# Layer 2 of a two-layer kernel on one core: the shifted copies of the values wait for the sorted rows, and four expert tiles' weights are fetched ahead of them

## The reference

```python
v = silu(causal_dwconv(hidden_states @ W_v, conv_w_v))        # q and k alike
vc = v.reshape(b, l, H * DV)
fir_s = causal_dwconv(vc, fir_short_w)      # 3 taps
fir_l = causal_dwconv(vc, fir_long_w)       # 31 taps
delta_out = delta_rule_chunkwise(q, k, v, beta)   # chunks of 32 rows, a scan over 8 chunks
gate_in = concatenate([hidden_states, fir_s, fir_l, delta_out], -1)
...
# experts: top 2 of 8 for every row
weights, indices = top_k(softmax(x @ router), 2)
out = sum over the two of  norm_weight * (silu(x @ gating[e]) * (x @ up[e])) @ down[e]
```

## Time and profile before

| | us |
|---|---|
| median of 3 runs | 667.78 (666.35 to 669.98) |
| profiled execution, first to last instruction (span) | 664.4 |
| PE busy | 517.5 (78%) |
| DVE busy | 423.6 (64%) |
| ACT busy | 223.4 (34%) |
| POOL busy | 208.5 (31%) |

### The profile page before, as it was taken

The page is one execution under the profiler, slowest core; times in us unless marked ns, Lnnn a source line. Parts: engine busy times, 40 slices in busy tenths (PEclk is TensorE's granted clock), DMA queues, the critical chain, the costliest instruction groups (busy, mean ns, idle before and its releaser), DMA issues.

```text
span 664.4 us, 17841 instructions
## 1 busy us (share of the span) xinstructions
PE 517.5 (78%) x7511; PEld 357.0 (54%) x7511; DVE 423.6 (64%) x861; ACT 223.4 (34%) x402; POOL 208.5 (31%) x170
## 2 busy tenths in 40 slices
PE   5636788888898889874869951789889889998962
PEld 4424566666666666652434420375458666656751
DVE  6897678686869696967456004947871123646796
ACT  2212444353344444350402102332222224424670
POOL 3472220303040404045512771382221111321470
PEclk9666799999999999998759995979995899898996
DMA  7375113131422332101100533154662343211216
GB/s 229 101 227 169 58 56 112 57 111 56 132 92 62 108 100 98 48 10 36 33 1 24 146 97 96 28 152 121 180 183 67 101 127 97 84 59 32 80 47 185
DMA packets 77838, 63.15 MB, mean 95 GB/s; under 512 B 9520, under 2 KB 70864, under 8 KB 77760
## 3 DMA queue, kind: packets, MB, share of 16 engines
q1 hardware_dynamic: 67840, 51.25, 26.6%
q0 software_dynamic: 3296, 7.02, 3.4%
q10 hardware_dynamic: 6624, 3.76, 2.1%
HBM read 44.42 MB, written 12.90 MB: 86 GB/s over the span
## 4 chain that ended last, share of the span: by engine, by line
PE 47%; DVE 18%; issue 10%; another core or an unknown queue 6%; ACT 5%; POOL 2%; DMA 1%; SPq 1%; DVEq 0%; ACTq 0%; POOLq 0%
PE ps L1045 5%; PE ps L874 5%; PE ps L914 4%; DVE small L1227 3%; PE ps L907 3%; DVE small L1190 3%; DVE BIG L1195 3%; PE ps L943 2%; PE ps L882 2%; PE ps L1054 2%; PE ps L769 2%; PE ps L822 2%; PE ps L732 2%; DVE BIG L1068 2%
## 5 line engine op out<-in xcount | busy, mean ns | idle before, releaser
L1863 POOL TENSOR_TENSOR BIG<-BIG,small 128x2048 f32<-128x2048 f32 x14 | 50.8, 3633 | 189.9 <-DVE small L1203 189.9
L1924 POOL DMA_INDIRECT home<-BIG x39 | 38.7, 992 | 140.0 <-ACT BIG L1806 125.0
L1068 DVE STREAM_TRANSPOSE BIG<-BIG 128x512 f32<-128x512 f32 (+3 forms) x30 | 25.6, 875 | 45.7 <-remote 44.9
L1045 PE MATMUL ps<-BIG 128*128 128x128 f32 x312 | 48.4, 305 | 3.3 <-ACT BIG L1638 3.3
L943 PE MATMUL ps<-BIG 128*32 128x512 f32 x256 | 32.5, 626 | 21.7 <-issue 21.7
L1045 PEld LDWEIGHTS ps<-BIG 128*128 128x128 f32 x312 | 43.9, 216 | 6.7 <-ACT BIG L1638 3.8
L874 PEld LDWEIGHTS ps<-BIG 128*128 128x128 f32 x368 | 44.7, 192 | 3.3
L874 PE MATMUL ps<-BIG 128*128 128x128 f32 x368 | 44.8, 275 | 0.0
L1694 ACT ACTIVATE BIG<-ps 128x1024 f32<-128x1024 f32 x32 | 31.0, 1022 | 36.6 <-PE ps L822 36.6
L1190 DVE TENSOR_REDUCE small<-ps 128x64 f32<-128x1024 f32 x32 | 39.0, 1219 | 6.2 <-PE ps L769 6.2
L1227 DVE TENSOR_REDUCE small<-ps 128x8 f32<-128x1024 f32 x32 | 37.7, 1219 | 7.9 <-PE ps L800 6.3
(11 more groups left out here) (264 smaller groups left out, 1114.9 us busy)
## 6 DMA issues: line engine op xcount, KB each, us to landing
BIG<-in_w SPq DMA_DIRECT2D x23, 512.0 KB
BIG<-in_w SPq DMA_DIRECT2D x23, 256.0 KB
BIG<-in_wg SPq DMA_DIRECT2D x39, 128.0 KB
BIG<-in_wu SPq DMA_DIRECT2D x39, 128.0 KB
BIG<-in_wd SPq DMA_DIRECT2D x39, 128.0 KB
BIG<-BIG SPq DMA_DIRECT2D x64, 71.4 KB
rows<-BIG SPq DMA_DIRECT2D x3, 936.0 KB
BIG<-rows ACTq DMA_DIRECT2D x39, 72.0 KB, 2.6
```

The source lines that it names most:

```text
L1045: t = e.matmul(bank(s)[:, i:i + 128], WT[(NTL[0] + j) % NWT][:, i:i + 128], XsT[(NTL[0] + j) % 2], start=True, stop=True)
L1068: return e.transpose(dst, src)
L1863: e.tensor_tensor(v, v, bc_last(zz[i], 16), ALU.mult).then_inc(p_ready, 1)
L1924: e.indirect_dma_start(YSd[1], bass.IndirectOffsetOnAxis(ap=XR[j % NXR][:, 128:129].bitcast(I32), axis=0), YS[J % 3], None).then_inc(d_hom ...
```

## The change

Two edits. The step `stack` gets one more wait, for all of the second 16 scatters. And SP's list is put in another order: `x1.2` and `x1.3` come ahead of all copies, the 16 DMAs of pair 0 come together ahead of the 16 of pair 1 (before, they alternated), and `x1.4`, `x1.5` and `x1.6` now stand each ahead of the copy that they stood behind. The list from `stack.2.3 x1.7` on is the same.

```diff
 TWO_SP = """
-x1.0 x1.1 stack.0.0 stack.1.0 x1.2 stack.0.1 stack.1.1 x1.3 stack.0.2 stack.1.2 stack.0.3 stack.1.3 stack.2.0 x1.4 stack.2.1 x1.5 stack.2.2
+x1.0 x1.1 x1.2 x1.3 stack.0.0 stack.0.1 stack.0.2 stack.0.3 stack.1.0 stack.1.1 stack.1.2 stack.1.3 x1.4 stack.2.0 x1.5 stack.2.1 x1.6 stack.2.2
...
                 if s[0] == "stack":
                     _, c, i = s
                     w.wait_ge(pad_ready, 1)
+                    w.wait_ge(d_scat[1], SCAT_ALL[1])
                     w.wait_ge(psum.empty(("pj", 2, c)))
                     if c >= 2:
                         w.wait_ge(psum.full(("fs", c - 2)))
```

More of the change, by code:

```diff
@@ L178 @@
 TWO_SP = """
-x1.0 x1.1 stack.0.0 stack.1.0 x1.2 stack.0.1 stack.1.1 x1.3 stack.0.2 stack.1.2 stack.0.3 stack.1.3 stack.2.0 x1.4 stack.2.1 x1.5 stack.2.2
-x1.6 stack.2.3 x1.7 x1.8 x1.9 stack.3.0 x1.10 stack.3.1 x1.11 stack.3.2 x1.12 stack.3.3 x1.13 x1.14 x1.15 x1.16 x1.17 x1.18 x1.19 x1.20
+x1.0 x1.1 x1.2 x1.3 stack.0.0 stack.0.1 stack.0.2 stack.0.3 stack.1.0 stack.1.1 stack.1.2 stack.1.3 x1.4 stack.2.0 x1.5 stack.2.1 x1.6 stack.2.2
+stack.2.3 x1.7 x1.8 x1.9 stack.3.0 x1.10 stack.3.1 x1.11 stack.3.2 x1.12 stack.3.3 x1.13 x1.14 x1.15 x1.16 x1.17 x1.18 x1.19 x1.20
 x1.21 x1.22 x1.23 x1.24 x1.25 x1.26 x1.27 x1.28 x1.29 x1.30 x1.31 x1.32 x1.33 x1.34 x1.35 x1.36 x1.37 x1.38
```

## The result

Over 16 runs of each kernel on one chip the changed kernel took 670.62 us (median; 666.98 to 677.74) and the kernel before 666.33 us (663.00 to 670.65). The ratio is 1.0067, with a 95% interval from 1.0040 to 1.0093: slower by 0.67%, some 4.5 us. The profiled execution has a span of 673.5 us against 664.4, 9.1 us apart, more than the medians are: this execution of the changed kernel took 675.60 us, 5.0 above its median. 0.9 us of the 9.1 lies ahead of the stage (the first scatter starts at 362.06, before at 361.16).

A forecast was written before the change was run, and what follows sets the result against it. Copies beside indirect scatters were taken to hold up semaphores. Terms +6.1, -1.9, -3.4, -3.5 to 0 and clock 0 gave +0.8 to -2.7, the queue +0.5 to -1.9; taken as 0: span 664.4, median 667.8, range 662.8 to 672.8.

The forecast's parts named there:

- rival B: At PE's projections: scatters alone hold signals; DVE still starts at 407.6, copies end 3.6 us later; 671.4; chance 0.15.
- The hold: At PE's projections: copies beside scatters hold semaphores; parting them lets DVE's block start at 391.3, 16.3 us earlier.
- The copies: After the scatters: 32 copies from 403.6, about 0.63 us apart; `fl.0.0` 2.3 us later, `fs.1` 6.1 later.
- From fs.1 to the first expert: From `fs.1` to `g1.1`: 6.7 us to `h1.0`, then 3.4 us of waits saved; `g1.1` 0.9 us late.
- the clock: One half-clock stretch moves from after `g1.1` to the filters, costing about 2.5 us there; net 0.
- The second hold: From `g1.1` to `gr.7`: ACT and DVE held again, DVE 3.47 us; may stay (0) or go (3.5 gained).
- SP's queue: Behind `x1.4`: down weights of `x1.7` issued at 455.2, so PE stands at `y1.5` until +0.5, or -1.9 without half clock.
- pair 1's +6.1: At `fs.1`: copies of pair 1 come after the scatters, so it starts at 425.3, 6.1 us later than 419.14.
- gains of 1.9 and 3.4: Between `fs.1` and `g1.1`: PE's 1.9 us wait for DVE goes, and 3.4 us of waits caused by ACT.

The follow-up runs named there:

- the plain stores on chip C: Kernel before with each of GpSimd's 32 indirect scatters replaced by a plain store of the same 128 rows to fixed places, rows unsorted; 646.40 us.
- chip C: Chip of the third group of follow-up experiments; the kernel before took 665.74 us there.
- the first comparison: The main result: changed kernel against the kernel before, 16 runs of each on one chip; 670.62 against 666.33 us, ratio 1.0067.
- chips A and C: Chips of the first and third groups of follow-up experiments; the kernel before took 668.54 us on A and 665.74 us on C.
- Chip B: Chip of the second group of follow-up experiments; the kernel before took 643.04 us there.
- the one with the pause: Kernel before with POOL waiting between the 16th and 17th scatter until PE has done the projection; 646.84 us, ratio 1.0034.

## Why the prediction was right or wrong

The time was forecast as 667.8 with a range from 662.8 to 672.8, and 670.62 was measured, inside the range and 2.8 above the likeliest value. Against the kernel before, with 666.33 over 16 runs, that is 4.5 us slower, more than the 3.3 us that the prediction took for no change. So the time was met and the mechanism was not: what happened is nearly rival B. That the time was met is in part luck, since the terms that went wrong were offset by others, as follows.

*The hold.* This step failed: "copies from SBUF to SBUF beside indirect scatters hold up semaphores". The scatters alone hold DVE; the copies add to ACT's hold and not to DVE's. The evidence in the profile of before was taken one way when it was open: the earlier trace rows show the second eight copies slow, and I read them as the cause where they were among the victims. What I had against it stood in the earlier trace rows: no transfer had been issued by SP from 388.6 until the fetch at 396.95, the share was low, and the hold went on. The 16.3 us that DVE's block was to be earlier were 0 (407.67 against 407.61 in the earlier trace rows). What they are worth where the hold does go is shown by the plain stores on chip C: DVE's block starts 30.4 us after the first store, and 46.4 us after the first scatter in the kernel before there, so 16.0 us sooner, and the kernel is 19.3 us shorter (one run at 646.40 against the median of 665.74). Stores that are over sooner may have a part in that; the hold is the most likely part of it, and no run parts the two. So the hold was the right thing to look at, and the change was not what removes it.

*The copies.* Right in kind and nearly in size. First copy 403.6 forecast, 404.37 measured; the piece of 32 in 20.87 us, 0.65 from one to the next, at the upper bound of 0.61 to 0.65; `fl.0.0` 415.2 and 416.05; `fs.1` 425.3 and 426.75. Rival B had put SP's release at 407.1, with the others', and its price for the copies at 3.6 us; SP was released 2.35 us after the last scatter began, like a landing of the earlier trace rows, and DVE 3.3 us after that; ACT's last eviction ahead of DVE's block had come before both. So B was right in the hold and too late by 2.7 us in the copies, and its 671.4 lies near the measured time also because the wait at `y1.5` and the low clock behind it made up for that.

*From fs.1 to the first expert, and the clock.* The 6.7 us of this step were 8.3 (426.75 to 435.07), and the saving of 3.4 us behind it was 3.9: from the transposition to `g1.1` PE took 3.54 us, against 7.39 before. The number is right for another reason than the one given. The prediction had PE's waits go because DVE would be done at 415.7. DVE was done at 431.85 as before; they went because PE came to these steps later, at 431.15 and after. The forecast of the clock held, in this profile. In the stretches of the changed kernel the granted clock is 0.58 for the filter behind `fs.1` (3.21 us against 1.90), after PE had waited 4.06 us, so mostly at 1.2 GHz of the two levels, and 1.00 from 435 to 440, where it was 0.50 before. It is no fixed price: in the kernel with the old end of the list PE waits 3.75 us at `fs.1`, and the filter behind it takes 1.90 us. What was not foreseen is the second row below, the filter behind the wait at `y1.5`:

```profile
427.70:431.20 3.50, 3.50 (x24) 0.69 (x19) 3.46 (x2) 0.00 (x0) 0.00 (x0) 0.58 0.00 0
461.70:465.00 3.30, 3.30 (x17) 0.55 (x16) 1.33 (x8) 0.39 (x2) 0.99 (x1) 0.53 0.66 202
435.00:440.00 5.00, 5.00 (x162) 4.44 (x151) 2.60 (x7) 3.78 (x8) 5.00 (x1) 1.00 0.18 46
```

*The second hold.* It did not stay as one long wait of DVE; PE's products came in bits at 443.3 to 446.1 and at 449.6 instead. From `g1.1` to `gr.7` it took 12.8 us. The sum had between 9.7 (14.7 less 2.5 less 3.5, plus 1) with this hold gone and 13.2 with it kept: it was kept, nearly whole.

*SP's queue.* This was named as what sets the rest, and it did, but at +3.4 instead of +0.5. The down weights of `x1.7` were issued at 458.56 and not 455.2: the fetch of `x1.4` began at 438.28 and not 436.8, its up weights took 1.69 us to issue and not 0.38, and the four copies behind it 3.41 and not 2.5. The PE wait itself (1.63 us) is small. Behind it the clock is low, which costs 1.5 us on the next 16 products, and no term of the sum had that. The two together are 3.1 of the +5.1. That the wait brings the low clock is not shown: on chip C it came behind one of 1.92 us in the changed kernel, and did not come behind one of 1.51 us at the same product in the kernel with all fetches behind the scatters:

```profile
467.81 0.49 PE L1056 MATMUL ps<-BIG 128*128 128x128 f32 x2 [1.51 <-DMA BIG<-in_wd]
...
468.56 1.92 PE L945 MATMUL ps<-BIG 128*32 128x512 f32 x16
```

*What it adds up to.* The sum had pair 1's +6.1 made good by gains of 1.9 and 3.4 and part of the second hold, and a queue at +0.5. Measured, +7.4 is made good down to +1.6 at `gr.7`, and the queue with the low clock brings it to +5.1. DVE's block stays where it was. In every kernel on a chip with the hold in which the scatters kept their place, it starts 5.4 to 7.7 us after the last of them. The chance of 0.15 for B was too small by what its own evidence said.

## What to carry to other kernels

If a slow stretch has two kinds of traffic in it, look for a stretch with one kind alone before saying that the mix is the cause, and price the change for each kind as the culprit. A wait that makes many DMAs start together moves a queue as a whole: follow the last entry that shares the queue, here a fetch of weights 50 us on, and look at the granted clock behind a gap in front of it. If the time of an unchanged kernel differs by several per cent from chip to chip, profile it beside the experiment; without that, three of these runs would have been read as proof of something they don't touch.

## What the runs showed of the hardware that was not expected

While GpSimd issued a row of indirect scatters (32, one each 1.26 us), other engines started their work late, at semaphores and between instructions. SP goes on to the copies 2.35 to 2.4 us after the last scatter's start, DVE only 5.4 to 7.7 us after it. The hold is there on chips A and C and in the first comparison. It begins some 7 to 18 us after the first scatter: in the changed kernel SP's issues are slow from 369 and ACT's evictions from 379.70, and with the scatters put off PE's products from 406. With no other transfer beside the scatters ACT's first late eviction is the one at 390.46, 28 us after the first.

Chip B shows nothing of it. The kernel before was not profiled there, but the one with the pause is the same up to its 16th scatter, with the same copies. From the end of the first eight copies to the next one its SP takes 2.56 us, where the kernel before took 6.80 in the first comparison, and the next eight are issued at full pace:

```profile
376.30 4.97 SPq L665 DMA_DIRECT2D BIG<-BIG  x8
```

So scatters and copies together are not enough for a hold either; something that differs between the chips, or between their states, must be added, and no run shows what. Nor does any show what is held inside the chip.

A long row is not needed. On chips A and C and in the first comparison PE's products come in bits again within 3 us of the start of POOL's first indirect store home (442.83 and 444.95 in the kernel before, 424.53 and 425.08 with the plain stores on chip C), and in none of the four profiles of chip B. This is the second hold of the prediction; copies of pair 2 are around it on all chips. The first layer's 16 scatters, at 30.70 to 51.83 us of the kernel before, show no such hold: DVE works on through most of them.
